# Denominators and block maxima in odd, unequal groups; normalisations with one tensor and two pointers, in a fused adaLN attention and FFN block

## The reference

```python
h = _layernorm(x) * (1 + ca) + sa
x = x + ga * attn(h)          # 16 heads of 64, causal
h = _layernorm(x) * (1 + cb) + sb
x = x + gb * ffn(h)           # 128 -> 352 -> 128

p = where(causal_mask, 0, exp(s - max(s)))      # s = (q * 64**-0.5) @ k.T
out = (p @ v) / (sum(p) + 1e-8)

scale = maximum(max(abs(xb)) / 6.0, 1e-12)      # xb: blocks of 16 columns
q = GRID[searchsorted(MID, abs(xb / scale))] * sign(xb) * scale   # before each FFN product
```

## Time and profile before

| what | us |
|---|---|
| median of 3 runs | 1278.59 |
| lowest and highest | 1277.71, 1278.70 |
| the profiled execution | 1277.56 |
| its span, first to last instruction | 1275.8 |
| PE busy | 1242.7 |
| DVE busy | 986.8 |
| ACT busy | 898.3 |
| POOL busy | 845.6 |

### The profile page before, as it was taken

The page is one execution under the profiler, slowest core; times in us unless marked ns, Lnnn a source line. Parts: engine busy times, 40 slices in busy tenths (PEclk is TensorE's granted clock), DMA queues, the critical chain, the costliest instruction groups (busy, mean ns, idle before and its releaser), DMA issues.

```text
span 1275.8 us, 33812 instructions
## 1 busy us (share of the span) xinstructions
PE 1242.7 (97%) x10194; PEld 1021.5 (80%) x10194; DVE 986.8 (77%) x2465; ACT 898.3 (70%) x2992; POOL 845.6 (66%) x1586
## 2 busy tenths in 40 slices
PE   6999999999999999999999999999999999999995
PEld 4778888888888888888888888788888788888774
DVE  5577877778777778777778787778787778787767
ACT  6676777776777777777777677777667777667761
POOL 4756666677666677666667666667666667666662
PEclk9999999999999999999999999999999999999996
DMA  3000000000000000000000000000000000000000
GB/s 105 20 20 24 17 8 23 23 23 23 13 10 23 23 23 22 11 12 23 23 23 22 9 14 23 23 23 21 7 17 23 23 23 21 6 19 23 19 22 9
DMA packets 38937, 26.53 MB, mean 21 GB/s; under 512 B 2913, under 2 KB 34145, under 8 KB 38913
## 3 DMA queue, kind: packets, MB, share of 16 engines
q1 hardware_dynamic: 38496, 25.96, 7.0%
q10 hardware_dynamic: 416, 0.26, 0.1%
HBM read 21.94 MB, written 4.28 MB: 21 GB/s over the span
## 4 chain that ended last, share of the span: by engine, by line
PE 95%; ACT 2%; DVE 2%; issue 1%; POOL 0%; DMA 0%; DVEq 0%; POOLq 0%; ACTq 0%
PE ps_m L1185 25%; PE ps_s L1287 19%; PE ps_m L1159 18%; PE ps_o L1318 14%; PE ps_m L1238 9%; PE ps_s L1298 5%; PE ps_m L1262 3%; ACT probs L690 1%; ACT qk L648 0%; PE ps_m L1409 0%; PE ps_s L1262 0%; ACT probs_t L644 0%; DMA x_in<-L_attn_x 0%; DVE neg_max L927 0%; DVE qy L62 0%
## 5 line engine op out<-in xcount | busy, mean ns | idle before, releaser
L690 ACT ACTIVATE probs<-ps_s,neg_max 128x128 f32<-128x128 f32 (+1 forms) x1024 | 423.4, 433 | 177.0 <-PE ps_s L1298 175.6
L469 POOL TENSOR_SCALAR probs<-probs,r_den 128x256 f32<-128x256 f32 (+1 forms) x768 | 354.0, 476 | 0.0
L927 DVE TENSOR_REDUCE neg_max<-ps_s 128x4 f32<-128x1024 f32 x256 | 305.7, 1215 | 61.1 <-PE ps_s L1287 61.1
L467 POOL TENSOR_TENSOR probs<-probs,r_den 128x128 f32<-128x128 f32 x256 | 107.1, 418 | 303.9 <-DVE r_den L938 289.7
L1287 PE MATMUL ps_s<-qk 64*128 64x256 f32 x2048 | 261.8, 394 | 1.8 <-ACT probs L690 1.8
L644 ACT COPY probs_t<-ps_m 128x512 f32<-128x512 f32 x287 | 167.6, 605 | 118.2 <-PE ps_m L1159 118.0
L1159 PE MATMUL ps_m<-ident,probs 128*128 128x128 f32 x1524 | 234.1, 277 | 5.8 <-ACT qk L648 3.6
L1287 PEld LDWEIGHTS ps_s<-qk 64*128 64x128 f32 x2048 | 181.1, 187 | 60.5 <-issue 24.0
L690 ACT ACTIVATION_READ_ACCUMULATOR probs<-ps_s,neg_max 128x1 f32 x1024 | 221.0, 216 | 0.0
L1159 PEld LDWEIGHTS ps_m<-ident,probs 128*128 128x128 f32 x1524 | 171.0, 140 | 38.3 <-ACT qk L648 13.3
L1318 PE MATMUL ps_o<-probs_t,v 128*64 128x256 f32 x2016 | 191.7, 332 | 0.0
(11 more groups left out here) (161 smaller groups left out, 1803.1 us busy)
## 6 DMA issues: line engine op xcount, KB each, us to landing
mod_a<-mod_rows SPq DMA_DIRECT2D x32, 256.0 KB, 3.3
x_res<-L_attn_x SPq DMA_DIRECT2D x32, 128.0 KB, 2.1
x_in<-L_attn_x SPq DMA_DIRECT2D x31, 128.0 KB, 2.1
out<-y_out SPq DMA_DIRECT2D x31, 128.0 KB, 1.8
mod_b<-mod_rows SPq DMA_DIRECT2D x31, 64.0 KB, 2.9
wkv<-L_attn_Wkv SPq DMA_DIRECT2D x3, 256.0 KB, 6.2
wo<-L_attn_Wo SPq DMA_DIRECT2D x1, 512.0 KB, 5.3
wkv<-L_attn_Wkv SPq DMA_DIRECT2D x2, 128.0 KB, 3.7
```

Of the source, the lines that this page charges most:

```text
L467: nc.gpsimd.tensor_tensor(cols, cols, r_den[:, u % 4, 0:1].to_broadcast([P, P]), ALU.mult)
L469: ins = nc.gpsimd.tensor_scalar(cols, cols, r_den[:, u % 4, s:s + 1], 1.0, ALU.mult, ALU.mult)
L690: ins = nc.scalar.activation(probs[:, u % 4, h, t * P:(1 + 2 * t) * P], ps_s[:, 2 * (u % 2) + h, t * N:t * N + (1 + t) * P], ACT.Exp, bias ...
L927: nc.vector.tensor_reduce(neg_max[:, u % 4, :], ps_s[:, 2 * (u % 2):2 * (u % 2) + 2, :].rearrange("p b (t j) -> p (b t) j", t=2), AX.X, AL ...
```

## The change

- `den` gets nine places for each unit's slot in place of four. The four sums stand in two groups of two with a gap behind each (places 0, 1, 3 and 4), and a third group (6, 7) holds nothing of use. L935 becomes an addition on three groups of two out of `den`, written to six adjacent places of `den_eps`. The reciprocal reads the first four of these.
- POOL fills `den` with 1.0 in an eighth setup step, since the unused places are read too. ACT waits for all eight steps ahead of its first DMA.
- The hidden rows' scales are made by a new function, `pair_scales`. Its maxima are written to `amax` as 11 groups of two with a gap, and the scales are read from these 11 groups and written to 22 adjacent places. The input of the FFN, the tail and the weights keep `quantize_scales`.
- `normalized` becomes a `tensor_scalar` with two per-partition pointers (mean and r) in place of a `scalar_tensor_tensor`, whose second tensor was r, repeated. This holds for all its callers.

```diff
+def pair_scales(nc, step, src, blocks, amax, scale, inverse):
+
+    pairs = amax[:, :].rearrange("p (a b) -> p a b", b=3)[:, :, 0:2]
+    step(nc.vector.tensor_reduce(pairs, src.rearrange("p (a b k) -> p a b k", b=2, k=BLOCK), AX.X, ALU.max,
+                                 apply_absolute_value=True))
+    step(nc.vector.tensor_scalar(scale[:, 0:blocks].rearrange("p (a b) -> p a b", b=2), pairs, 1.0 / 6.0, 1e-12,
+                                 ALU.mult, ALU.max))
+    step(nc.vector.reciprocal(inverse[:, 0:blocks], scale[:, 0:blocks]))
...
-        den = sb("den", [P, 4, 4])
-        den_eps = sb("den_eps", [P, 4, 4])
+        den = sb("den", [P, 4, 9])
+        den_eps = sb("den_eps", [P, 4, 6])
...
-        amax = [sb(f"amax{n}", [P, I // BLOCK]) for n in range(3)]
+        amax = [sb(f"amax{n}", [P, 3 * I // BLOCK // 2]) for n in range(3)]
...
-        POOL_SETUP = 7
+        POOL_SETUP = 8
...
+            init(nc.gpsimd.memset(den[:, :, :], 1.0))
...
+            act.wait_ge(pool_setup, POOL_SETUP)
             act.dma_start(x_in[:, :, :], x_v[0]).then_inc(x_loaded, 16)
...
-                                bias=neg_max[:, u % 4, s:s + 1], accum_out=den[:, u % 4, s:s + 1])
+                                bias=neg_max[:, u % 4, s:s + 1], accum_out=den[:, u % 4, 3 * h + t:3 * h + t + 1])
...
-                    nc.vector.scalar_tensor_tensor(dst[t], src[:, t, :], mv[:, t, 0:1], r[:, t:t + 1].to_broadcast([P, P]),
-                                                   ALU.subtract, ALU.mult).then_inc(ready, 1)
+                    nc.vector.tensor_scalar(dst[t], src[:, t, :], mv[:, t, 0:1], r[:, t:t + 1], ALU.subtract, ALU.mult).then_inc(ready, 1)
...
-                    quantize_scales(nc, Steps(dve, hq_steps[k], QUANT_STEPS, b), hh[:, k, :], I // BLOCK, amax[k + 1],
+                    pair_scales(nc, Steps(dve, hq_steps[k], QUANT_STEPS, b), hh[:, k, :], I // BLOCK, amax[k + 1],
...
-                    nc.vector.tensor_scalar(den_eps[:, u % 4, :], den[:, u % 4, :], SOFTMAX_EPS, None,
+                    nc.vector.tensor_scalar(den_eps[:, u % 4, :].rearrange("p (a b) -> p a b", b=2),
+                                            den[:, u % 4, :].rearrange("p (a b) -> p a b", b=3)[:, :, 0:2], SOFTMAX_EPS, None,
                                             ALU.add).then_inc(eps_added, 1)
...
-                    nc.vector.reciprocal(r_den[:, u % 4, :], den_eps[:, u % 4, :]).then_inc(rden_ready, 1)
+                    nc.vector.reciprocal(r_den[:, u % 4, :], den_eps[:, u % 4, 0:4]).then_inc(rden_ready, 1)
```

More of the change, by code:

```diff
@@ L1109, in _ @@
             dve.wait_ge(exp_done, 16 * B)
-            nc.vector.tensor_scalar(den_eps[:, 3, :], den[:, 3, :], SOFTMAX_EPS, None, ALU.add).then_inc(eps_added, 1)
+            nc.vector.tensor_scalar(den_eps[:, 3, :].rearrange("p (a b) -> p a b", b=2),
+                                    den[:, 3, :].rearrange("p (a b) -> p a b", b=3)[:, :, 0:2], SOFTMAX_EPS, None,
+                                    ALU.add).then_inc(eps_added, 1)
             dve.wait_ge(eps_added, UNITS * B)
-            nc.vector.reciprocal(r_den[:, 3, :], den_eps[:, 3, :]).then_inc(rden_ready, 1)
+            nc.vector.reciprocal(r_den[:, 3, :], den_eps[:, 3, 0:4]).then_inc(rden_ready, 1)
             dve.wait_ge(xqt_high, 1)
```

## The result

The changed kernel takes **1282.97 us** (median of 7 executions, 1281.9 to 1283.49). The kernel before, on the same chip, takes 1278.52 (7 executions, 1277.71 to 1278.7). The ratio is 1.0035, with an interval of 1.0026 to 1.0045. So it is slower by 4.4 us, where no change was forecast, and the time lies outside the forecast range. The profiled execution took 1281.9 us with a span of 1280.2, which is 4.4 above the span of before, at a mean granted clock of 0.992.

What follows compares the result with a forecast made beforehand. PE was taken to bound the kernel, busy 1098.69 of 1100 us. Start +2.4, tail -0.25, xn in bodies -2.5 and part 1 +0.5 gave +0.15 on 1278.59, so 1278.7 us (no change), range 1276.6 to 1281.6.

Steps and rivals of the forecast that it cites:

- the term for sharing in the start: Start: x_in's transfer, sharing the engines with SP's weights, was to take 0.3 us longer, bounds 0 and about 0.8.
- The issue at 3.1: Start: ACT, waiting for POOL's setup, was to issue x_in at 3.1 in place of 0.73, 2.37 us later.
- nothing covers the start: Start: x_in's DMA heads the chain with no other work to cover it; with sharing, everything comes 2.67 us later.
- The two pointers: Start and tail: xn's normalisation pair was to take some 0.37 us for 0.62, so -0.25 us in each.
- xn in the bodies: Bodies: den_eps, no longer held by POOL, lets xn come earlier; PE regains 0.10 us in 28 bodies, taken as -2.5.
- The order in part 1: Bodies, part 1: POOL's multiply gets in between, maxima(4) come 0.12 to 0.17 us later; 0.02 a body, +0.5 in all.
- The lock-turn rival: Bodies, part 1: DVE's quotients lose two turns to POOL, PE 0.1 us a body; +2.8, 1281.5 us; chance 0.15.
- The slower side: Bodies: DVE losing two turns (1281.5, chance 0.15) or xn gaining nothing (1281.2, chance 0.12); slower in all 0.20.
- The range's lower end: Whole kernel: 1276.6 us, said to take in all of xn's gain, a start of 2.0 and no loss in part 1.
- That the change doesn't do what it says: Bodies: groups counted as written, so den_eps stays 0.35 and L55 0.82 us; time 1278.2; chance 0.10.

## Why the prediction was wrong

It gave +0.15 us and the measurement is +4.4. The step that failed is the term for sharing in the start. By its steps:

- **The start's sharing term failed.** "Its 128 KB are 0.4 us at 306 GB/s, so sharing costs 0 at best and about 0.8 at worst; I take 0.3, because at 3 to 5 us the queues are only filling." It cost 3.4 us (5.79 against 2.4), which is 3.1 of the 4.3 us of error. The queues weren't only filling: SP's packets took 68.6% of the engines from 2.0 to 4.5 us. And the worst case of 0.8 took `x_in` to keep a large part of the rate. While it moved, both of ACT's loads together got 0.24 MB in 3.96 us, 61 GB/s, and SP's got 196. By 3.06 us SP had issued five loads and was at the sixth. The timeline of the changed kernel's start has the last of the five, ACT's issue, and the sixth:

```profile
2.60 0.43 SPq L403 DMA_DIRECT2D wkv<-L_attn_Wkv  x1
...
3.06 0.46 ACTq L632 DMA_DIRECT2D x_in<-L_attn_x  x1
3.07 0.43 SPq L404 DMA_DIRECT2D wkv<-L_attn_Wkv  x1
```

The run in which SP waits too shows 2.39 us for the same load at the same time of issue. The bytes that SP has under way while the load moves, 0.78 MB against 0.14 before, were what had to be counted. The trace of before had a hint that I didn't use: SP's loads of 128 KB behind others took 3.7 us, where `x_in`, among the first, took 2.4.
- **The issue at 3.1** was right (3.06). So was the claim that nothing covers the start: first maxima 5.80 later with `x_in` 5.7 later.
- **The two pointers were mis-priced.** I took 0.37 us for the pair against 0.62. It takes 0.60 (10.96 in the chain above). The form with pointers costs what the old one costs, and the immediate form from which I estimated (L1056, 225 ns) is another. So the -0.25 in the start and the -0.25 in the tail were worth 0.02 each (the last xn2's pair takes 0.60 for 0.62). What the form does bring is that a neighbour holds it less: beside POOL the means are 382 and 473 ns (417 and 499 before), and PE gains 0.05 a body by it alone.
- **xn in the bodies: the mechanism right, the size half.** The place, the cause (`den_eps` held by POOL) and the 0.10 that PE gains there are as forecast, and so is `den_eps` at 0.15. What I left out was the question what is late next: the wait for ACT's exponentials, 1.8 us behind, takes back 0.045. I had also counted on the addition alone, and each of the three edits by itself brings the same gain, by the wait at xn. The bodies together measured -1.36 us, for -2.5 + 0.5 = -2.0 in the sum, and their period is 38.31 for the 38.28 forecast.
- **The order in part 1** went exactly as worked out (L64 at 0.18, the sum waiting for L87, maxima of unit 4 later by 0.12), and it cost less than I took. `hq`'s transposes come 0.10 later, and the next step of PE is back to within 0.02 of its old time, since it waited for ACT's copy anyway. The lock-turn rival fell, with its place right and its price covered.
- **The rivals.** The slower side was named (1281.5, 1281.2), each time for a mechanism in the bodies. None was a start worse than its bound, which the range only left outside as a case without a price. The range's lower end doesn't follow from its own terms either: a start of 2.0, the tail, all of xn's gain and no loss in part 1 give 1277.5, not 1276.6. That the change doesn't do what it says fell too: the odd, unequal groups do free the operation, although their destination rows touch. The Trainium skill (VectorE: DVE Perf Modes, "Mode 2×_2P — use both read ports for one tensor") names the outermost counts, even, or odd and equal, as what lets a one-source operation take both ports. The three forms of the same addition agree with it: 0.15 us for odd and unequal, 0.36 for each of the other two.

## What to carry to other kernels

A wait put ahead of the first load of a queue can cost more than its own length: here the load lost its place ahead of what the other queue issues in the meantime, 2.3 us of waiting made 5.7. Count the bytes that other queues will have under way while the late load moves, and put such a wait right ahead of the first instruction that needs it. And where a stall goes, follow PE to the next thing it waits for before the stall's whole length is counted: here nearly half came back 1.8 us later, and three different remedies for one stall gave together no more than the cheapest gave alone.

## What the runs showed that I had not expected

- The packets of two queues were shared far more evenly than their bytes: 398 packets of ACT's against 537 of SP's in the same 4.5 us, 0.25 against 0.92 MB. Here the queue with the small packets got the small share of the bytes.
- Starting all loads 2.3 us late (SP and ACT both waiting) beats starting SP's on time and ACT's late by 3.7 us.
- A change of order alone, the pairs, took the hold off an operation that it doesn't touch: `den_eps` in its old form takes 0.16 when it starts 0.03 us behind POOL's multiply, and 0.35 when 0.15 behind, each in 28 bodies.
- Two kernels with the same bodies differ by 0.02 us a body from execution to execution. That is as much as the parts of this change differ from each other, so single profiles can't rank them.
